# Rotary halves exchanged by VectorE's output partitions in place of a second, swapped base projection

## What is computed

```python
xn = (x - mu) / jnp.sqrt(var + EPS) * ln_w + ln_b
uv = jax.nn.silu(xn @ uv_w.T + uv_b)
u, v, base = (uv[..., :E], uv[..., E:2 * E], uv[..., 2 * E:])      # 256, 256, 128 wide
base = base[:, :, None, :] * gamma[None, None] + beta              # two rows of gamma, beta
base = _rope(base)                 # [x1*cos - x2*sin, x2*cos + x1*sin] over the two halves of 64
q, k = (base[:, :, 0, :], base[:, :, 1, :])
qk = jnp.einsum('bis,bjs->bij', q, k)
kernel = jnp.square(jax.nn.relu(qk / SQRT_S + bias[None]))
out = u * jnp.einsum('bij,bje->bie', kernel, v)
return out @ o_w.T + o_b + shortcut
```

## Time and profile before

| what | us |
|---|---|
| median of 3 runs | 392.43 |
| lowest, highest | 391.45, 393.58 |
| the profiled execution, its own time | 391.36 |
| span of its instructions | 389.5 |
| the seven turns ahead of the expert loop | from about 20 to 208 |
| the expert loop | from about 208 to 357 |
| turn 7, sums and stores | from about 357 to 389.5 |

### The profile page before, as it was taken

How to read it: one execution, slowest core, us unless ns; L and a number is a source line. 1 busy time by engine, 2 the same in 40 slices (tenths; PEclk the granted TensorE clock), 3 DMA queues, 4 the chain that set the end, 5 groups by cost and what they waited for, 6 DMA issues and landing times.

```text
span 389.5 us, 6982 instructions
## 1 busy us (share of the span) xinstructions
PE 351.0 (90%) x1984; PEld 269.4 (69%) x1985; DVE 275.1 (71%) x646; ACT 228.4 (59%) x418; POOL 171.0 (44%) x161
## 2 busy tenths in 40 slices
PE   1779979989989999999996999999999999999791
PEld 1565658556556565756644989899899999998540
DVE  3879465789997774947643776777777777776876
ACT  0774996474653756646363767676676666772610
POOL 3004600000076377677760265666656566667000
PEclk9989999999999999999996999999999999999997
DMA  6999300000014811111112354544444446521795
GB/s 159 307 276 257 70 0 2 0 0 3 0 42 126 268 48 48 37 55 48 50 48 68 98 158 120 160 129 143 156 130 148 137 135 156 140 84 49 202 301 151
DMA packets 56836, 43.88 MB, mean 113 GB/s; under 512 B 6673, under 2 KB 49041, under 8 KB 56817
## 3 DMA queue, kind: packets, MB, share of 16 engines
q1 hardware_dynamic: 50304, 32.71, 32.6%
q0 software_dynamic: 4544, 9.38, 6.7%
q10 hardware_dynamic: 1968, 1.55, 1.3%
HBM read 26.36 MB, written 17.26 MB: 112 GB/s over the span
## 4 chain that ended last, share of the span: by engine, by line
PE 53%; DVE 16%; DMA 10%; ACT 10%; issue 6%; POOL 2%; ACTq 1%; DVEq 1%; SPq 0%
PE bank L1284 11%; DMA slot_x<-slots_in 9%; PE bank L1021 8%; PE bank L1115 8%; PE bank L1023 7%; PE bank L1022 7%; ACT base_qk L484 3%; PE bank L1101 3%; PE bank L1121 3%; PE bank L1261 2%; DVE work L762 2%; DVE work L756 2%; PE bank L1078 1%; ACT work L446 1%; ACT work L497 1%
## 5 line engine op out<-in xcount | busy, mean ns | idle before, releaser
L1008 POOL DMA_INDIRECT results<-work,dest x78 | 90.4, 1159 | 67.5 <-issue 22.4
L993 POOL DMA_INDIRECT slots_in<-work,slot_i x64 | 65.4, 1022 | 87.8 <-issue 62.6
L1284 PE MATMUL bank<-wdn,work 128*128 x624 | 76.1, 275 | 0.1
L1284 PEld LDWEIGHTS bank<-wdn,work 128*128 128x128 f32 x624 | 73.0, 192 | 0.3 <-issue 0.3
L1115 PE MATMUL bank<-kern,v 128*128 128x512 f32 x128 | 58.7, 592 | 0.0
L593 ACT ACTIVATE work<-bank 128x512 f32<-128x512 f32 x78 | 46.6, 600 | 6.5 <-PE bank L1023 3.9
L1021 PE MATMUL bank<-sx_lo,w_hi 128*128 128x256 f32 x156 | 48.3, 310 | 1.4 <-DVE w_lo L900 1.4
L1022 PE MATMUL bank<-sx_hi,w_lo 128*128 128x256 f32 x156 | 44.6, 286 | 0.0
L1023 PE MATMUL bank<-sx_hi,w_hi 128*128 128x256 f32 x156 | 44.5, 285 | 0.0
L584 ACT CAST sx_hi<-bank 128x256 fp32r<-128x256 f32 x39 | 14.5, 373 | 43.9 <-PE bank L1261 43.9
L906 DVE TENSOR_TENSOR work<-work 128x512 f32<-128x512 f32 x39 | 27.1, 694 | 18.7 <-ACT work L593 18.7
(11 more groups left out here) (163 smaller groups left out, 671.2 us busy)
## 6 DMA issues: line engine op xcount, KB each, us to landing
region<-in_L_ffn_W_up SPq DMA_DIRECT2D x39, 256.0 KB, 2.8
slots_in<-zeros SPq DMA_DIRECT2D x1, 5148.0 KB, 24.7
slot_x<-slots_in SPq DMA_DIRECT2D x39, 132.0 KB
region<-results SPq DMA_DIRECT2D x12, 256.0 KB, 5.0
wdn<-in_L_ffn_W_down SPq DMA_DIRECT2D x4, 512.0 KB, 6.3
out<-x_all SPq DMA_DIRECT2D x8, 256.0 KB, 2.3
results<-work,dest POOLq DMA_INDIRECT x78, 3.4
x_all<-in_L_attn_x SPq DMA_DIRECT2D x2, 512.0 KB, 7.6
```

Source lines behind the costliest of these rows:

```text
L993: pool.indirect_dma_start(slots_in, bass.IndirectOffsetOnAxis(slot_i[:, k, t:t + 1], 0), xs1[:, t, at], None, element_offset=k * 2).then_i ...
L1008: pool.indirect_dma_start(results, bass.IndirectOffsetOnAxis(dest[:, at:at + 1], 0), slot_y[:, k, :], None).then_inc(returned[k], 16)
L1284: last = pe.matmul(P_Y[half][:, 0:D], hid_t[:, h, c, half * P:(half + 1) * P], wdn[:, of, c, :].rearrange("p a d -> p (a d)"), start=(c == ...
```

## The change

The swapped copy of the base goes, with all that fed it. The product "bsw", its Silu and two of the four scalings are no longer made. The swapped loads of the weights, the bias, gamma and beta go too. The multiplication by the sines becomes two instructions of 64 partitions each: one reads partitions 64 to 127 and writes 0 to 63 of `rot2`, the other the reverse, and the signs in the sine table are exchanged to fit. "bsw" is no longer in `RING`, so the slots of a turn are one fewer and some products wait for another reader than before.

```diff
-UVC = 768
-BASE, BSW = 512, 640
+UVC = 640
+BASE = 512
-    c[:, C_SIN:C_SIN + T] = np.concatenate([-np.sin(angle), np.sin(angle)])
+    c[:, C_SIN:C_SIN + T] = np.concatenate([np.sin(angle), -np.sin(angle)])
...
-        RING = [("x1", 0), ("x2", 0), ("base", 0), ("bsw", 0), ("rt", 0)]
+        RING = [("x1", 0), ("x2", 0), ("base", 0), ("rt", 0)]
...
-                RING += [("x2", b + 1), ("base", b + 1), ("bsw", b + 1), ("x1", b + 1)]
+                RING += [("x2", b + 1), ("base", b + 1), ("x1", b + 1)]
...
-            for dst, dst_sw, src in ((gam, gam_sw, gamma), (bet, bet_sw, beta)):
-                for to, of in ((dst[:, :], src), (dst_sw[0:HALF, :], src[:, HALF:S]), (dst_sw[HALF:S, :], src[:, 0:HALF])):
-                    sp.dma_start(to, of.rearrange("a s -> s a"), allow_slow_non_contiguous=True).then_inc(ld["turn_cols"], 16)
+            for dst, src in ((gam, gamma), (bet, beta)):
+                sp.dma_start(dst[:, :], src.rearrange("a s -> s a"), allow_slow_non_contiguous=True).then_inc(ld["turn_cols"], 16)
...
-            cols(uvb_c[0:HALF, 3:4], uv_b[2 * EU + HALF:2 * EU + S].rearrange("(p a) -> p a", a=1))
-            cols(uvb_c[HALF:S, 3:4], uv_b[2 * EU:2 * EU + HALF].rearrange("(p a) -> p a", a=1))
...
-            act.dma_start(uv_raw[:, 0:5, :], uv_w.rearrange("(c p) h -> p c h", p=P)).then_inc(ld["uv"], 16)
-            act.dma_start(uv_raw[0:HALF, 5, :], uv_w[2 * EU + HALF:2 * EU + S]).then_inc(ld["uv"], 16)
-            act.dma_start(uv_raw[HALF:S, 5, :], uv_w[2 * EU:2 * EU + HALF]).then_inc(ld["uv"], 16)
+            act.dma_start(uv_raw, uv_w.rearrange("(c p) h -> p c h", p=P)).then_inc(ld["uv"], 16)
...
             def base_silu(b):
                 act.wait_ge(qk_made, START + b)
-                act.wait_ge(base_made, START + b * 4)
-                for n, name in enumerate(("base", "bsw")):
-                    act.activation(silu_b[:, n, :], of_ring(name, b), ACT.Silu, bias=uvbias[:, 2 + n:3 + n])\
-                       .then_inc(silu_b_made, 1)
-                for n, (by, plus) in enumerate(((gam, bet), (gam_sw, bet_sw))):
-                    act.wait_ge(silu_b_made, START + b * 2 + (n + 1))
-                    for k in range(2):
-                        act.activation(base_qk[:, n, k, :], silu_b[:, n, :], ACT.Identity, bias=plus[:, k:k + 1], scale=by[:, k:k + 1])\
-                           .then_inc(base_made, 1)
+                act.wait_ge(base_made, START + b * 2)
+                act.activation(silu_b[:, :], of_ring("base", b), ACT.Silu, bias=uvbias[:, 2:3]).then_inc(silu_b_made, 1)
+                act.wait_ge(silu_b_made, START + b + 1)
+                for k in range(2):
+                    act.activation(base_qk[:, k, :], silu_b[:, :], ACT.Identity, bias=bet[:, k:k + 1], scale=gam[:, k:k + 1])\
+                       .then_inc(base_made, 1)
...
             def rotate_base(b):
-                dve.wait_ge(base_made, START + b * 4 + 2)
+                dve.wait_ge(base_made, START + b * 2 + 2)
                 dve.wait_ge(qk_lo_made, START + b)
-                dve.tensor_tensor(rot1, base_qk[:, 0], cos_sin[:, 0:1, :].broadcast_to([P, 2, T]), ALU.mult)\
+                dve.tensor_tensor(rot1, base_qk[:, :, :], cos_sin[:, 0:1, :].broadcast_to([P, 2, T]), ALU.mult)\
                    .then_inc(rot1_made, 1)
-                dve.wait_ge(base_made, START + b * 4 + 4)
-                dve.tensor_tensor(rot2, base_qk[:, 1], cos_sin[:, 1:2, :].broadcast_to([P, 2, T]), ALU.mult)\
-                   .then_inc(rot2_made, 1)
+                for to, of in ((slice(0, HALF), slice(HALF, S)), (slice(HALF, S), slice(0, HALF))):
+                    dve.tensor_tensor(rot2[to], base_qk[of], cos_sin[of, 1:2, :].broadcast_to([HALF, 2, T]), ALU.mult)\
+                       .then_inc(rot2_made, 1)
             def rotate_sum(b):
                 dve.wait_ge(rot1_made, b + 1)
-                dve.wait_ge(rot2_made, START + b + 1)
+                dve.wait_ge(rot2_made, START + b * 2 + 2)
                 dve.tensor_tensor(rot1, rot1, rot2, ALU.add).then_inc(qk_made, 1)
...
-            for c in range(2):
-                last = pe.transpose(banks[5][:, c * P:(c + 1) * P], uv_raw[:, 4 + c, :], ident)
-            last.then_inc(uv_turned, 1)
+            pe.transpose(banks[5][:, 0:P], uv_raw[:, 4, :], ident).then_inc(uv_turned, 1)
...
             def base_part(b):
                 pe.wait_ge(x2_lo_made, START + b + 1)
                 uv_part("base", b, BASE)
-                uv_part("bsw", b, BSW)
```

More of the change, by code:

```diff
@@ L108, in build @@
         cos_sin = sb("cos_sin", [P, 2, T])
-        base_qk = sb("base_qk", [P, 2, 2, T])
+        base_qk = sb("base_qk", [P, 2, T])
         bias_t = sb("bias_t", [P, BIAS_W])
@@ L127, in build @@
         xs1 = cut(0, (NT, ROW_W))
-        silu_b, ut, vf = [cut(N_ROWS + k * 1024, (2, T)) for k in range(3)]
+        silu_b, ut = cut(N_ROWS, (T,)), cut(N_ROWS + 1024, (2, T))
         vf = cut(N_ROWS + 2048, (TB, EU))
@@ L148, in build @@
         st = early_cut(1024, (NT, 6))
-        uv_raw, ow_raw = early_cut(2944, (6, P)), early_cut(2944 + 768, (2, P))
-        lnb_row, uv_lnb = early_cut(1216, (P,)), early_cut(2176, (4, P))
+        uv_raw, ow_raw = early_cut(2944, (5, P)), early_cut(2944 + 768, (2, P))
+        lnb_row, uv_lnb = early_cut(1216, (P,)), early_cut(2176, (3, P))
         spare_g = g[:, :, :].rearrange("p t d -> p (t d)")
@@ L171, in build @@
         lnw_c, lnb_c, ob_c = sb("lnw_c", [P, 1]), sb("lnb_c", [P, 1]), sb("ob_c", [P, 1])
-        uvb_c, uvbias = sb("uvb_c", [P, 4]), sb("uvbias", [P, 4])
+        uvb_c, uvbias = sb("uvb_c", [P, 3]), sb("uvbias", [P, 3])
         vb_bc = sb("vb_bc", [P, EU])
-        gam, gam_sw = sb("gam", [P, 2]), sb("gam_sw", [P, 2])
-        bet, bet_sw = sb("bet", [P, 2]), sb("bet_sw", [P, 2])
+        gam, bet = sb("gam", [P, 2]), sb("bet", [P, 2])
         wr = sb("wr", [P, NE])
@@ L249, in build @@
             if b == 0:
-                RING += [rt[1], ("x2", 1), rt[2], ("base", 1), ("bsw", 1), rt[3], ("x1", 1), rt[4]]
+                RING += [rt[1], ("x2", 1), rt[2], ("base", 1), rt[3], ("x1", 1), rt[4]]
             elif b < LAST:
-                RING += [("x2", b + 1), ("base", b + 1), ("bsw", b + 1), ("x1", b + 1)]
+                RING += [("x2", b + 1), ("base", b + 1), ("x1", b + 1)]
             if b >= LAST - 1:
@@ L424, in _ @@
             act.wait_ge(zeros_set, 1)
-            act.activation(silu_b[:, 0, 0:1], zeros[:, 0:1], ACT.Silu).then_inc(silu_loaded, 1)
+            act.activation(silu_b[:, 0:1], zeros[:, 0:1], ACT.Silu).then_inc(silu_loaded, 1)
             def turned_weights():
@@ L566, in _ @@
             act.wait_ge(uvb_made, 1)
-            act.wait_ge(ld["turn_cols"], 6 * 16)
+            act.wait_ge(ld["turn_cols"], 2 * 16)
             base_silu(0)
@@ L868, in _ @@
                                      ALU.mult, ALU.subtract).then_inc(uvw_made, 1)
-            dve.wait_ge(ld["uv"], 3 * 16)
+            dve.wait_ge(ld["uv"], 16)
             dve.wait_ge(ld["lnb"], 16)
@@ L872, in _ @@
             dve.tensor_tensor(uv_lnb[:, 0:2, :], uv_raw[:, 0:2, :], by_lnb, ALU.mult).then_inc(uvb_parts, 1)
-            dve.tensor_tensor(uv_lnb[:, 2:4, :], uv_raw[:, 4:6, :], by_lnb, ALU.mult).then_inc(uvb_parts, 1)
+            dve.tensor_tensor(uv_lnb[:, 2:3, :], uv_raw[:, 4:5, :], by_lnb[:, 0:1, :], ALU.mult).then_inc(uvb_parts, 1)
             dve.wait_ge(uvb_parts, 2)
             dve.tensor_reduce(uvbias[:, :], uv_lnb, AX.X, ALU.add).then_inc(uvb_parts, 1)
-            dve.wait_ge(ld["cols"], 4 * 16)
+            dve.wait_ge(ld["cols"], 2 * 16)
             dve.wait_ge(uvb_parts, 3)
@@ L1026, in _ @@
             pe.wait_ge(ld["ident"], 16)
-            pe.wait_ge(ld["uv"], 3 * 16)
+            pe.wait_ge(ld["uv"], 16)
             for c in range(4):
                 pe.transpose(banks[4][:, c * P:(c + 1) * P], uv_raw[:, c, :], ident)
-            for c in range(2):
-                last = pe.transpose(banks[5][:, c * P:(c + 1) * P], uv_raw[:, 4 + c, :], ident)
-            last.then_inc(uv_turned, 1)
+            pe.transpose(banks[5][:, 0:P], uv_raw[:, 4, :], ident).then_inc(uv_turned, 1)
             def output_weights():
@@ L1056, in routing_counted @@
                 pe.matmul(P_ROUTE[:, NT * NE:2 * NT * NE], ones[:, :], picks, start=True, stop=True).then_inc(counted, 1)
-            READ = {"x2": (x2_lo_made, 1, 1), "x1": (x1_lo_made, 1, 1), "base": (silu_b_made, 2, 1), "bsw": (silu_b_made, 2, 2),
+            READ = {"x2": (x2_lo_made, 1, 1), "x1": (x1_lo_made, 1, 1), "base": (silu_b_made, 1, 1),
                     "v0": (v_biased, 2, 1), "v1": (v_biased, 2, 2), "u0": (ut_made, 2, 1), "u1": (ut_made, 2, 2), "fin": (mixed, 1, 1)}
```

## The result

The changed kernel took 396.99 us as the median of four runs (396.26 to 400.08), the kernel before 392.56 (391.45 to 393.58). The ratio is 1.0146, with a 95% interval of 1.0105 to 1.0187. So the change costs about 1.5%, clear of the noise. The forecast was 396.7, slower. The profiled execution took 396.58 with a span of 394.7, against 391.36 and 389.5 before. The two profiled executions differ by 5.2, the two medians by 4.4.

A forecast was written before the change was run, and what follows sets the result against it. It took the ACT and DVE path to v0, nearly equal to PE's, as the bound. Work terms 3.0 + 1.5 - 1.8 - 0.7 + 1.4 = +3.4, plus 0.9 for the clock, gave +4.3: 396.7 us by the median, range 393.2 to 400.0.

The forecast's parts named there:

- PE's share: Steady turn, base product to v0: removing "bsw" (0.70 us) moves nothing; PE's wait of 0.17 grows to 0.87.
- Rival 4: PE's 0.70 counts in every turn, as its 90% busy time suggests: 387.5 us; chance 0.03.
- ACT's share: Same stretch: with one Silu instead of two, scalings start 0.73 after it and the cosine product 0.47 us earlier.
- DVE's share: Sine product as two 64-partition halves: each lasts 1.22 us like the full one, with starts 1.26 apart.
- Rival 3: Half height saves DVE time, with 0.65 per half; sends then late next: 389.6 us, faster; chance 0.07.
- rival 1: Halves overlap like any two instructions, 1.13 us for each start: 393.6 to 394.6 us; chance 0.17.
- A steady rotation: Rotations b = 2, 4, 5, 6: ACT's saving and DVE's extra starts sum to +0.75 us each on the path to v0.
- b = 3: Rotation where DVE is full with routing: ACT's saving counts for nothing, so +1.5 us.
- b = 1: Turn 0 to 1, where ACT is full: nearly all of ACT's saving is kept, -1.8 us, the only large gain.
- The ring, the sends: New ring-slot readers were done microseconds earlier, and POOL's last send stays hidden ahead of the loop: no cost.
- The clock: PE's longer waits may drop the granted clock: one lost stretch taken, partly in idle time, +0.9 us; bounds 0 and +4.5.
- rival 2: Clock lost in two or three of the long waits, 1.5 us each: about 399 to 400 us; chance 0.20.

The follow-up runs named there:

- in-place halves: Changed kernel with each half of the sine product writing the partitions it reads, halves not exchanged: 400.17 us in one execution.
- dummy products: Changed kernel with eight matmuls of 512 columns into an unused PSUM bank in turn 7, between sh1 and v0: 397.00 us, ratio 1.0145.
- one sine product: Changed kernel with one full-height sine product in place of the two halves, halves not exchanged: 387.64 us, ratio 0.9881.
- the second tile in the kernel before: Kernel before with a second tile for the Silu of u and that Silu ahead of the cast on ACT: 390.94 us, ratio 0.9928.
- with it in the changed kernel: Changed kernel with a second tile for u's Silu, that Silu ahead of the cast: 394.43 us; also with x1_lo ahead of the halves: 394.69 us.

## Why the prediction was right

The direction, the size and the mechanism came out. Step by step:

- **PE's share** (nothing). Right: steady turns grew to 24.24, and PE waits 1.40, against a forecast of 1.6; the other 0.2 is ahead, at sh0. Rival 4 falls.
- **ACT's share** (-0.47). Right: Silu to scalings 0.72 for a forecast of 0.73.
- **DVE's share** (1.22 a half, 1.26 a start). Right, by the dearer bound. Rival 3 (height saves time) falls with 1220 ns, rival 1 (all starts overlap) with 1.26 and 1.25. The in-place halves show why: two of those three starts would have been held even without an exchange.
- **A steady rotation** (+0.75). +0.76, +0.73 and +0.76 in turns 2, 5 and 6. In turn 4 it is +1.04, because v0 of turn 3 ran at the low clock: its fourth matmul starts 0.77 behind its first, with a normal distance of 0.46.
- **b = 3** (+1.5). +1.50 from the cosine product to v0. The marker shows 0.29 more, because DVE's work of turn 2 ended that much later against v0. The first thing on DVE to be late there is the reader of v0's product, 1.44 behind v0's start and 1.08 before. It is no accident of one execution: 1.44 or 1.45 stands in turn 2 of the halves in place, of the kernel before with its sine split and of both executions with dummy products, and 1.08 in the kernel with one sine product. Why stays open.
- **b = 1** (-1.8). -1.45. ACT's saving itself was right. But its work from 40 on starts 0.37 later than before (the cast of x_hi at 40.54 for 40.17), because the granted clock stayed at 0.50 up to about 32 in turn 0, where it was back at 30.3 in the kernel before. The step took PE's turn 0 as unchanged, though PE's wait ahead of the first scores was bound to grow from 2.04: the products in front of it ended 1.5 earlier.
- **b = 0** (nothing). The first qk_lo starts at 25.46 where it started at 25.57: -0.11, within the forecast's 0.3.
- **End of turn 6** (-0.7): -0.77. **b = 7** (+1.4): +1.36, and PE's idle 3.61 for a forecast of 3.6.
- **The ring, the sends** (nothing). No wait shows for a ring slot, and the first slot transpose waits for DVE's sum of the rows (x_all), not for the sends (208.28 and 211.14). The last send moved by -0.45 (201.42), less than the -1.05 of the forecast. In the kernels that shortened the turns the sends did become the next bound, as rival 3 had said of them.
- **Not in the sum**: the loop is 0.58 shorter. Nothing in the change touches it. From the first slot transpose to the cosine product behind the loop it is 149.16 before and 148.58 after, and 150.23 and 149.49 in the two executions with dummy products, which have the same loop. So 0.58 is within what the loop varies by. And sh0's wait for x1_lo, which the prediction did not see, although the kernel before shows it in turn 3 (3.05 from sh0 at 109.31 to v0 at 112.36). It cost no time, since v0 hangs on the longer path, but it split the idle stretches of turns 2 and 3 into 1.21 and 1.38, and 2.08 and 0.40, where one of 2.8 and one of 3.6 had been forecast.
- **The clock** (+0.9). The term that was mis-sized most: 0.4 in turn 0, 0.3 in turn 3 and 1.6 in turn 7, 2.2 in the profiled execution. The prediction left out turn 0. Its condition of rival 2 came true in this execution, since the clock was lost behind two of the three long waits, but not rival 2's price of 1.5 for each: in turn 3 most of it fell into idle time. The step argued from the length of a wait, and that argument fell: the same wait of 1.8 lost the clock once and kept it once, and so did the same 2.08. Within one kernel the slower executions tend to be those with the lower mean granted clock: the kernel with one sine product took 384.66 at 0.985 and 389.59 at 0.968, the changed kernel 396.26 at 0.973 and 400.08 at 0.966. It is not the whole spread, for the kernel before took 391.21 at 0.982 and 395.60 at 0.983. Which stretch loses the clock in which execution stays open.

So the mechanism on DVE and ACT was right, and that the median came within 0.3 of the forecast is partly luck. In the profiled execution the work terms of 3.4 came to 3.54 (0.29 more ahead of b = 3, a little less elsewhere), the clock took 2.24 for 0.9, and the loop gave 0.58: 5.2, where +4.3 had been forecast. By the medians it was +4.4, because the profiled execution before lay 1.2 under its median and the one after only 0.4.

## What to carry to other kernels

An instruction of half the height is not half an instruction: price VectorE by length along the partition, and add the 0.12 us measured here for each start that moves between partitions 0 and 64 against the instruction ahead. Work taken off the busiest engine is worth nothing where that engine waits; find the one stretch in which two paths meet (here PE against ACT and DVE, 0.17 us apart), and price the change on the longer of them. After a gain, ask what fixed chain is next: here 64 sends of POOL, 93.5 to 99.5 us in the profiled executions, for which PE waited in every kernel that shortened the turns (1.77 to 4.43).

## What was not expected of the hardware

- The clock is not a function of the idle time just ahead. Idle stretches of 1.79 and 2.20 us lost it, 1.81 and 2.24 kept it, and one of 2.08 did both in two executions of the same program. A stretch at 0.50 in which PE is fully busy cost 1.56 to 1.6 us in turn 7.
- The held start has a sharp edge. Behind a product of the same length the next starts after 1.14 or after 1.25, by nothing but the partition at which they begin.
- The 64 sends took 94.5 us in the kernel before and in the changed kernel, 93.5 with one sine product, 95.2 with the second tile in the kernel before, and 98.1 and 99.5 with it in the changed kernel, though POOL's instructions were the same.
